# DLRM tower on one core: table look-ups by matmul widened from 256 to 512 columns, in four classes of tables

## The reference

```python
e = jnp.stack([tbl_0[ids[:, 0]], ..., tbl_25[ids[:, 25]]], axis=1)          # 2048 x 26 x 128
all_vecs = jnp.concatenate([dense_proj[:, None, :], e], axis=1)
interactions = jnp.einsum('bnd,bmd->bnm', all_vecs, all_vecs)
rows, cols = np.triu_indices(27, k=1)
z = jnp.concatenate([dense_proj, interactions[:, rows, cols]], axis=1)
h = jnp.concatenate([z, dense_proj], axis=1)
h = jnp.maximum(h @ W_top1 + b_top1, 0.0)                                   # 607 -> 512
h = jnp.maximum(h @ W_top2 + b_top2, 0.0)                                   # 512 -> 256
y = h @ W_top3                                                              # 256 -> 1
```

## Time and profile before

| | |
|---|---|
| median of 3 runs | 379.75 us (379.35 to 380.21) |
| the profiled execution's own time | 379.39 us |
| its span | 377.5 us |
| TensorE matmuls busy | 344.4 us (91%) |
| VectorE busy | 239.1 us (63%) |
| ScalarE busy | 143.7 us (38%) |
| GpSimd busy (gathers) | 244.8 us (65%) |
| mean granted TensorE clock | 0.985 of 2.4 GHz |
| DMA | 35.86 MB, mean 95 GB/s |

### The profile page before, as it was taken

How to read it: one execution, slowest core, us unless ns; L and a number is a source line. 1 busy time by engine, 2 the same in 40 slices (tenths; PEclk the granted TensorE clock), 3 DMA queues, 4 the chain that set the end, 5 groups by cost and what they waited for, 6 DMA issues and landing times.

```text
span 377.5 us, 14444 instructions
## 1 busy us (share of the span) xinstructions
PE 344.4 (91%) x6144; PEld 321.1 (85%) x6144; DVE 239.1 (63%) x702; ACT 143.7 (38%) x256; POOL 244.8 (65%) x260
## 2 busy tenths in 40 slices
PE   0774997979999999999999999999999999999897
PEld 0674996969988998999999998999999998998786
DVE  4989998685564876658665876658564975602300
ACT  2274331434423443525313443535413452536122
POOL 5357777777777777777777777777767777670000
PEclk9999899898999999999999999999999999999999
DMA  7999823242414232242324242232413122110000
GB/s 193 290 255 246 259 66 124 56 132 61 126 51 134 52 118 62 56 125 63 118 56 123 51 113 68 54 119 56 125 44 130 48 56 56 49 49 9 5 2 0
DMA packets 17702, 35.86 MB, mean 95 GB/s; under 512 B 6605, under 2 KB 9677, under 8 KB 17679
## 3 DMA queue, kind: packets, MB, share of 16 engines
q0 software_dynamic: 8192, 16.79, 16.7%
q1 hardware_dynamic: 8335, 18.72, 16.4%
q10 hardware_dynamic: 1152, 0.01, 0.2%
HBM read 35.49 MB, written 0.01 MB: 94 GB/s over the span
## 4 chain that ended last, share of the span: by engine, by line
PE 85%; DMA 7%; issue 2%; DVE 2%; POOL 2%; SPq 2%; ACT 0%; DVEq 0%; POOLq 0%
PE hid L395 13%; PE gram L424 12%; PE look_ps L351 8%; PE look_odd L351 8%; PE vec_act L312 8%; PE look_odd L353 8%; PE look_ps L353 7%; PE hid L402 7%; PE hid L351 4%; PE hid L353 4%; DMA vecs<-tbl,ids_sb 3%; DMA raw<-tbl 3%; POOL vecs L295 2%; PE small L414 1%; PE small L364 1%
## 5 line engine op out<-in xcount | busy, mean ns | idle before, releaser
L295 POOL DMA_INDIRECT vecs<-tbl,ids_sb x256 | 244.6, 955 | 94.6 <-issue 78.0
L572 DVE TENSOR_SCALAR onehot<-step_ids,row_no 125x256 fp32r<-125x256 int32 x640 | 196.4, 376 | 86.7 <-PE look_odd L353 38.0
L547 ACT COPY vecs_T<-vec_act 128x512 f32<-128x512 f32 x64 | 46.5, 733 | 112.1 <-PE vec_act L312 111.9
L351 PE MATMUL look_odd<-onehot,look_hi 125*128 125x256 f32 x256 | 67.9, 302 | 5.1 <-DMA vecs<-tbl,ids_sb 2.6
L351 PE MATMUL look_ps<-onehot,look_hi 125*128 125x256 f32 x256 | 67.8, 300 | 1.6 <-DVE look_lo L580 1.6
L353 PE MATMUL look_ps<-onehot,look_lo 125*128 125x256 f32 x256 | 63.7, 284 | 0.0
L353 PE MATMUL look_odd<-onehot,look_lo 125*128 125x256 f32 x256 | 63.6, 285 | 0.0
L424 PE MATMUL gram<-vecs_T 128*27 128x26 f32 x4096 | 52.4, 192 | 3.7 <-issue 1.2
L424 PEld LDWEIGHTS gram<-vecs_T 128*27 128x27 f32 x4096 | 44.1, 104 | 13.2 <-issue 6.8
L351 PEld LDWEIGHTS look_odd<-onehot,look_hi 125*128 125x128 f32 x256 | 49.2, 192 | 5.9 <-DVE look_lo L580 2.8
L351 PEld LDWEIGHTS look_ps<-onehot,look_hi 125*128 125x128 f32 x256 | 49.3, 193 | 2.2 <-DVE look_lo L580 1.8
(11 more groups left out here) (74 smaller groups left out, 288.9 us busy)
## 6 DMA issues: line engine op xcount, KB each, us to landing
step_ids<-look_ids SPq DMA_DIRECT2D x15, 640.0 KB
raw<-tbl SPq DMA_DIRECT2D x10, 448.0 KB
vecs<-tbl,ids_sb POOLq DMA_INDIRECT x256
vecs<-dense SPq DMA_DIRECT2D x16, 64.0 KB, 1.8
raw<-tbl SPq DMA_DIRECT2D x10, 52.0 KB
step_ids<-look_ids SPq DMA_DIRECT2D x1, 512.0 KB
w_sb<-w SPq DMA_DIRECT2D x1, 512.0 KB
raw<-w_dense SPq DMA_DIRECT2D x1, 512.0 KB, 10.4
```

The lines of the kernel that those rows point to most:

```text
L295: nc.gpsimd.indirect_dma_start(out=vecs[j][:, 1 + k, :], out_offset=None, in_=tables[k], in_offset=bass.IndirectOffsetOnAxis(ap=ids_sb[:, ...
L351: nc.tensor.matmul(bank, look_hi[:, f, ch, :], onehot[:, i % SLOTS, c, :], start=ch == 0, stop=False)
L547: return engine_copy(vecs_T[j][:, :, lo:lo + GROUP], bank[:, :, :].rearrange("d v b -> d b v"))
L572: last = nc.vector.tensor_scalar(onehot[:, i % SLOTS, c, :], step_ids[a][0:LOOK_K, f - a * LOOKUPS // 2, :], row_no[0:LOOK_K, ch:ch + 1], ...
```

## The change

A look-up matmul now moves 512 columns, four tiles, with the same weights. To spread this work evenly, the ten tables stand in four classes of 2, 3, 2 and 3 tables (`CLASS_TABLES`). Class c is looked up in tile 4r+c, for the four tiles 4r+c+1 to 4r+c+4; so each tile still has ten units, each of 2 chunks (4 matmuls) and 512 columns, and a table has four units. In the prologue (round -1) class c gets c+1 tiles: 128, 256, 384 or 512 columns; in the last round class c gets 3-c. ScalarE copies a table's first tile straight to `vecs_T` and the other three to `looked`, and merges three classes in each tile. Two PSUM banks take turns by table.

The raw tables have a place of their own each, the memory in which their low part will stand, so SyncE loads all ten without waiting. Ids are loaded a table at a time, into four slots. Dense rows come features-first from the host, which takes away their transposes; the output layer has its weights as the small operand, 256 columns. The gathers wait for look-ups of the same number of tables as before. VectorE's and ScalarE's loops are unrolled; TensorE's runs over rounds of four tiles. `h1_T`, `h2_T` and the output row have their own buffers.

```diff
-UNIT_CH = LOOK_CH // 2
-RAWS = 4
+UNIT_CH = 2
+UNITS = LOOK_CH // UNIT_CH
+SPAN = 4
+WIDE = SPAN * P
+CLASS_TABLES = (2, 3, 2, 3)
+CLASS_FIRST = (0, 2, 5, 7)
+    def group(r, f):
+        c = class_of(f)
+        first = SPAN * r + c + 1
+        return max(first, 0), min(first + SPAN, tiles)
...
-        raw = [sb(f"raw{k}", [P, LOOK_CH * D]) for k in range(RAWS)]
+        with nc.sbuf_tensor("raw", [LOOK_K, LOOKUPS, LOOK_CH, D], F32) as raw:
+            pass
+        look_lo = sb("look_lo", [LOOK_K, LOOKUPS, LOOK_CH, D], F32R)
+        wide_ids = sb("wide_ids", [P, IDS_SLOTS, WIDE], I32)
+        onehot = sb("onehot", [LOOK_K, SLOTS, UNIT_CH, WIDE], F32R)
+        looked = sb("looked", [D, LOOKUPS, SPAN - 1, P])
...
                 def load_table(f):
-                    if f >= RAWS:
-                        sp.wait_ge(table_split, f - RAWS + 1)
...
+                load_ids(-1, 3)
+                for f in range(3, LOOKUPS):
+                    load_table(f)
+                for f in range(4, LOOKUPS):
+                    load_ids(-1, f)
...
-                            pool.wait_ge(onehot_used, SLOTS * (2 * t + k // HALF_GATHERS))
+                            pool.wait_ge(onehot_used, LOOKUPS * (2 * t + k // HALF_GATHERS))
...
-                    nc.tensor.transpose(dense_ps, vecs[j][:, 0, :], ident[:, :]).then_inc(dense_turned, 1)
...
+                def look_up(r, f, part, count):
+                    n = number(r, f)
+                    if isinstance(r, int) and r < 0 and part == 0:
+                        pe.wait_ge(table_split, f + 1)
+                    pe.wait_ge(onehot_made, UNITS * n + part + 1)
+                    if part == 0 and positive(n - 1):
+                        pe.wait_ge(looked_up, n - 1)
+                    slot = (UNITS * f + part) % SLOTS
+                    bank = look_ps[f % 2][:, 0:count * P]
+                    for c in range(UNIT_CH):
+                        ch = part * UNIT_CH + c
+                        nc.tensor.matmul(bank, look_hi[:, f, ch, :], onehot[:, slot, c, 0:count * P],
+                                         start=ch == 0, stop=False)
+                        last = nc.tensor.matmul(bank, look_lo[:, f, ch, :], onehot[:, slot, c, 0:count * P],
+                                                start=False, stop=ch == LOOK_CH - 1)
+                    last.then_inc(onehot_used, 1)
...
-                    for h in range(2):
-                        for c in range(H2 // P):
-                            last = nc.tensor.matmul(bank[:, h:h + 1], h2_T[:, c, h * P:(h + 1) * P], w3_sb[:, c:c + 1],
+                    for c in range(H2 // P):
+                        last = nc.tensor.matmul(bank, w3_sb[:, c:c + 1], h2_T[:, c, :],
...
+                for f in range(LOOKUPS):
+                    for part in range(UNITS):
+                        make_unit(-1, f, part)
+                    take_low(f)
...
+                    direct = nc.scalar.copy(vecs_T[first % 2][:, :, col], look_ps[f % 2][:, 0:P])
+                    nc.scalar.copy(looked[:, f, slot:slot + count - 1, :].rearrange("d k b -> d (k b)"),
+                                   look_ps[f % 2][:, P:count * P]).then_inc(looked_up, 1)
```

## The result

The changed kernel takes **396.53 us** (median of four runs, 394.97 to 399.39), beside 379.98 for the kernel before: a ratio of 1.0445, 95% interval 1.0406 to 1.0484. The forecast was 379.0, from 371.5 to 383.5. So it is slower by 4.5%, and outside the range. The profiled execution took 396.62 us, 1.82 above its span of 394.8.

A forecast was written before the change was run, and what follows sets the result against it. TensorE bound the middle, GpSimd 2.3 us a round behind; after the change #24 sets the time. #24 at 49.4, gathers 290.4, 2.93 to data, tail 34.1: span 376.8, about 379.0 us as median, range 371.5 to 383.5.

The forecast's parts named there:

- 231 gathers at 1.257: GpSimd's gathers from #24 to the last, #255, each 1.257 us from start to start: 290.4 us.
- unless: VectorE beside GpSimd: skill's rule says no contention outside 2-port modes; the rows disagree, unless these one-hots use such a mode.
- #24: Gather 24 counted from 0, second half of tile 1, in the prologue: forecast start 49.1 us, bounds 47.3 to 53.4.
- rival (2): Prologue: wait before table 4 leaves TensorE at 1.2 GHz; #40 waits 8 us, up to 388; chance 0.25 with rival (3).
- #40's gate: Gather 40, second half of tile 2, waits for tile 0's first quarter of interaction matmuls: 69.5 us, adding 0.3.
- 512 columns a matmul: TensorE's look-ups: one of 512 columns starts each 0.217 us, saving 1.8 us a round of two tiles.
- rival (3): TensorE stays the bound, 512 columns at 0.24 us or more; 384 us at 0.25; chance 0.25 with rival (2).
- the 5.3 us that I let the gathers win: GpSimd's waits for TensorE from #24 to the last gather, all that faster TensorE rounds could take off the kernel.
- The tail: From the transposes needing the last gather to the end: 33.3 us before, forecast 34.1.
- Put at nothing: Terms priced at zero: loads of dense rows and ids in the loop, ScalarE's copies and merges, low parts in place.
- The signs named ahead: Profile signs: VectorE idle about 20 to 29 us, #24 at 47 to 53, no GpSimd wait over 0.5 us after #40.
- the last gather at 337 to 344: Sign on GpSimd: the last gather falls at 337 to 344 us; the sum had it start at 339.8.

The follow-up runs named there:

- Experiment 4: Kernel before, one VectorE instruction building two chunks' one-hots (2 x 256 elements), look-ups still 256 columns, output not the reference's: 393.13 us, ratio 1.0374.
- experiment 2: Changed kernel with each 512-column one-hot built in two instructions of 256, matmuls still 512 columns wide: 394.90 us, ratio 1.0378.
- experiment 3: Changed kernel with ids of tables 4 and 5 issued earlier and one-hots of at most 256 columns: 388.37 us, ratio 1.0218.
- experiment 7: The version of experiment 3 with TensorE's loop over rounds of four tiles written out: 381.68 us, ratio 1.0037.
- experiment 8: Changed kernel with only TensorE's loop over the rounds written out: 396.79 us, ratio 1.0455.
- experiment 9: Kernel before with TensorE's loop body holding four tiles instead of two, same instructions in the same order: 391.72 us, ratio 1.0316.
- experiment 11: Kernel before with dense rows features-first from the host and output-layer weights as the small operand: 380.58 us, ratio 0.9988.
- experiment 6: Changed kernel with each one-hot instruction cut into pieces of 128 columns: 403.37 us, ratio 1.0623.
- experiment 10: Kernel before with TensorE's loop over the pairs of tiles written out: 381.29 us, ratio 1.0043.

## Why the prediction was wrong, step by step

- **The step that failed is "231 gathers at 1.257".** I carried the spacing over as if it were GpSimd's own. It is that of GpSimd beside one-hots of 256 columns; beside 512 it is 1.311, which is 12.5 of the 18.0 us by which the span was missed. Experiment 4 shows this cause alone, experiment 2 its absence. The rows had shown the pair from VectorE's side (3.24 us a table against 3.74). I scaled that with the columns and didn't ask what the longer instruction does to the gather. The Trainium skill ("SBUF — State Buffer", Who interferes with whom) also says that `tensor_scalar` can enter a 2-port mode, in which it and GpSimd shut each other out for a whole instruction; I had named that with an "unless" and given it no price. That all gathers over 1.1 us overlap one-hots fits such a lock, but that it is this lock isn't shown. What is left open is why one-hots of 256 columns do the gathers no harm where 512 do, and what the low part adds in the prologue. Of the 12.5 us about 1.2 belong to the gathers beside low parts.
- **#24.** The forecast was 49.1 (47.3 to 53.4) and it came at 53.16, inside the bounds. The mechanism was right, the place of the ids in the queue. They were there at 31.46, 2.5 us later than taken, and from there to #24 it was 21.7 us, not 20.1. The granted clock was 0.63 from 30 to 40 us and 0.89 from 40 to #24, so table 4's matmuls didn't bring TensorE back at once, as I had it. Of rival (2) that part came true, but not its sign (from 45 us to #24 the granted clock was 1.00) and not its 8 us at #40.
- **#40's gate.** It came at 75.82 and not at 69.5, 22.7 us behind #24 instead of 20.1, with no wait in between: longer gathers again.
- **512 columns a matmul.** 0.217 us was too low; it is 0.22 to 0.23, and from the first look-up of a unit to the second it is 0.3 or more in 26 of 40 units of two full rounds. In the changed kernel the gathers hide it. With the gathers at their old length it counts: full rounds take 41.7 and 42.4 us in experiment 3 and 41.6 to 42.5 in experiment 7, not 40.2. Two full rounds counted from each matmul's start to the next show which terms failed: the look-ups take 40.4 us in both experiments where they took 41.8 before, so a round saves 0.7 us and not 1.8; the interaction matmuls take 14.7 and 15.5 us where they took 14.0; the transposes save 0.2 a round, and the output layer nothing. So rival (3), TensorE as the bound, was nearer to the truth than the forecast wherever the one-hots are narrow, and the 5.3 us that I let the gathers win were hardly there.
- **TensorE's loop.** No step looked at the length of its body. In the changed kernel this costs nothing (experiment 8), but 6.7 us in experiment 3 and 11.9 in experiment 9, where gathers wait for TensorE.
- **The tail.** 36.2 us, not 34.1: the first layer took 1.7 more at the lower clock, behind a wait for the last gathers, and the gap of issue in the last interaction was 2.45 us, where the kernel before has one of 1.18 at 356.06.
- **Put at nothing:** the loads in the loop, ScalarE's work and the low parts in place end no wait on GpSimd behind #24. The dense rows and the output layer gave nothing by themselves (experiment 11).
- **The signs named ahead.** VectorE's wait for the ids, #24 at 47 to 53, no wait on GpSimd behind #40 and look-ups each 0.22 us were met or just missed, and the time was wrong by 17.5 us. None of these signs was the length of a gather; the only one that depended on it, the last gather at 337 to 344, failed (356.03). TensorE's wait for gathers at each even tile's third group failed too: it waited at 89.59, 101.15, 109.88 and 153.20 and then not before the last gathers (358.57), since its own rounds, 41 us and not 40.2, were hardly faster than the longer gathers.

In the medians, one upon the other: the changed kernel 396.5, with the ids in time 390.0, with one-hots in halves 388.4, with the loop written out 381.7, with whole one-hots in the prologue 378.65. That is 1.2 us under the kernel before (379.80): all that these experiments got out of the wide look-ups. The steps depend on their order, and the one from 390.0 to 388.4 is hardly clear of the noise.

## What to carry to other kernels

The spacing of an engine's instructions is measured beside its neighbours: where a change widens a neighbour's instruction, price the pair from both sides, even if the neighbour's total falls. Where two engines are within some 5% of each other, undoing one fault shows little until the next is undone too, so try them together as well as alone. And where work is regrouped over more tiles, look at what grows with the group outside the arithmetic: the load that the first one waits for, and the length of the loop's body.

## What the runs showed of the hardware

- One-hots of 512 columns (`tensor_scalar`, int32 to fp32r) lengthen the indirect gathers in the changed kernel from 0.951 to 1.005 us in the mean, and to 1.28 at most where no low part is near; in pieces of 256 columns the mean is 0.954. One of 512 takes 503 ns in the mean, two of 256 take 756.
- The longest gathers stand in the prologue, at a low part (`tensor_tensor` of 125x1024, both inputs in SBUF, 1.2 us): 1.99 us in the changed kernel, 1.95 with one-hots of at most 256 columns (experiments 2, 3 and 7), and 3.21 in experiment 4 with wide one-hots before and behind it. Others beside a low part take 0.94 (kernel before, experiment 2), so the moment of the start plays a part; which, wasn't tested.
- A TensorE loop whose body is four tiles stops for 2.9 to 4.5 us, put down to issue, where it goes back (the shortest, 2.92, in experiment 6 at 240.78); with a body of two tiles it doesn't. The instruction queue moved 45 packets in the changed kernel, 52 in experiment 9 and 18 in the kernel before, so I read the stop as a body that must be loaded anew. When the packets move fits this: in the kernel before there is none from 128.9 to 344.4 us, most of its loop; in experiment 9 they go on through the whole loop, and one starts at 172.5 and one at 260.5 us, just as the two stops begin (172.38 and 260.47). Straight code moves about as many (48 in experiment 10) and shows no such stop.
- Behind a stop of 3.9 or 4.5 us the granted clock is 0.59 over the next 5.6 or 6.3 us of full work, which makes the stop cost 5 to 6 us.
